# VectorE's and ScalarE's order in the last block of the first FFN

## The reference

```python
c  = cond(x)            # x @ W.T + 2 * (gated rank-16 LoRA, top 2 of 8 experts)
a  = sum_m term_m(c) @ fuse_m.T + approx_up(c) @ local.T
f  = (silu(c @ gate.T) * (c @ up.T)) @ down.T        # first FFN, 1248 hidden features
x1 = x + a + f
d  = x1 @ W2.T + b2 + 2 * (x1 @ A[slot]) @ B[slot]   # LoRA chosen per sequence
h1, h3 = lora_linear(d, w1), lora_linear(d, w3)      # second FFN, 1376 hidden features
out = x1 + lora_linear(silu(h1) * h3, w2)
```

## Time and profile before

| | |
|---|---|
| median of 3 runs | 448.58 us (448.51 to 448.97) |
| the profiled execution | 448.42 us |
| its span in the trace | 446.7 us |
| TensorE busy | 441.4 us, 99% |
| VectorE busy | 324.0 us, 73% |
| ScalarE busy | 212.2 us, 48% |
| TensorE's granted clock | 1.00 throughout |

### The profile page before, as it was taken

One profiled execution on the slowest core, in us unless ns is written; L12 is line 12 of the kernel. 1 busy time (PEld: TensorE's weight loads), 2 busy tenths in 40 slices (PEclk: granted clock), 3 DMA queues, 4 the chain that ended last, 5 costly groups with the idle time before them and its releaser, 6 DMA issues.

```text
span 446.7 us, 5568 instructions
## 1 busy us (share of the span) xinstructions
PE 441.4 (99%) x2009; PEld 363.5 (81%) x2009; DVE 324.0 (73%) x471; ACT 212.2 (48%) x324; POOL 29.3 (7%) x51
## 2 busy tenths in 40 slices
PE   8999999999999999999989999999999999999997
PEld 6788888888888888888778888888888888888886
DVE  5756699667989688896899248989853568887631
ACT  6364452345757447564565527365541124654300
POOL 1004100000001100005200000000000000000000
PEclk9999999999999999999999999999999999999999
DMA  8406800044574655657340010222201122121022
GB/s 301 132 0 195 201 0 1 12 119 117 117 190 118 147 133 121 145 138 198 109 150 6 18 48 18 70 66 61 74 2 41 57 91 66 48 66 53 1 102 87
DMA packets 20299, 40.44 MB, mean 91 GB/s; under 512 B 2672, under 2 KB 4736, under 8 KB 20272
## 3 DMA queue, kind: packets, MB, share of 16 engines
q1 hardware_dynamic: 16992, 32.51, 22.6%
q0 software_dynamic: 3280, 7.58, 9.7%
HBM read 37.98 MB, written 2.10 MB: 90 GB/s over the span
## 4 chain that ended last, share of the span: by engine, by line
PE 95%; DVE 3%; DMA 1%; ACT 0%; issue 0%; ACTq 0%
PE PS L1697 16%; PE PS L1698 16%; PE PS L1699 16%; PE PS L1562 15%; PE PS L1563 15%; PE PS L1564 15%; PE PS L1874 1%; DVE WU L938 1%; DMA X<-in_x 1%; DVE X L1180 1%; PE PS L1576 0%; PE PS L1922 0%; PE PS L1932 0%; PE PS L1933 0%; DVE S L1249 0%; DVE G L938 0%
## 5 line engine op out<-in xcount | busy, mean ns | idle before, releaser
L1697 PE MATMUL PS<-HT,WU 128*128 128x512 f32 x266 | 103.9, 391 | 1.3 <-DVE T L1123 1.0
L1698 PE MATMUL PS<-HT,WU 128*128 128x512 f32 x266 | 103.6, 389 | 0.0
L1699 PE MATMUL PS<-HT,WU 128*128 128x512 f32 x266 | 103.6, 389 | 0.0
L503 ACT ACTIVATE WU<-raw 128x256 fp32r<-128x256 f32 (+2 forms) x55 | 49.0, 897 | 31.0 <-PE PS L1699 15.1
L1697 PEld LDWEIGHTS PS<-HT,WU 128*128 128x128 f32 x266 | 50.0, 188 | 12.7 <-DVE T L1123 1.4
L938 DVE TENSOR_TENSOR WU<-raw,WU 128x256 fp32r<-128x256 f32 (+2 forms) x56 | 56.5, 1014 | 5.1 <-ACT WU L503 5.0
L1699 PEld LDWEIGHTS PS<-HT,WU 128*128 128x128 f32 x266 | 49.9, 188 | 10.5
L503 ACT ACTIVATE PS<-PS 128x512 f32<-128x512 f32 x46 | 26.8, 582 | 66.0 <-PE PS L1699 59.0
L1698 PEld LDWEIGHTS PS<-HT,WU 128*128 128x128 f32 x266 | 50.0, 188 | 10.0
L938 DVE TENSOR_TENSOR G<-T,G 128x1024 fp32r<-128x1024 f32 (+2 forms) x46 | 43.9, 967 | 12.2 <-ACT G L503 11.6
L503 ACT ACTIVATE G<-T 128x1024 fp32r<-128x1024 f32 (+2 forms) x47 | 39.8, 856 | 22.0 <-DVE T L1054 6.8
(11 more groups left out here) (170 smaller groups left out, 713.1 us busy)
## 6 DMA issues: line engine op xcount, KB each, us to landing
raw<-in_pieces SPq DMA_DIRECT2D x73, 256.0 KB, 3.0
raw<-in_parts SPq DMA_DIRECT2D x14, 512.0 KB, 3.6
raw<-in_parts POOLq DMA_DIRECT2D x14, 384.0 KB, 5.0
X<-in_x SPq DMA_DIRECT2D x8, 256.0 KB, 4.9
raw<-in_pieces SPq DMA_DIRECT2D x14, 128.0 KB, 2.8
out_x<-X SPq DMA_DIRECT2D x7, 256.0 KB, 2.0
su_raw<-in_stk_up POOLq DMA_DIRECT2D x6, 192.0 KB, 2.6
T<-in_lora_b POOLq DMA_DIRECT2D x16, 32.0 KB, 2.5
```

The source lines that it names most:

```text
L503: return nc.scalar.activation(o, i, ACT.Copy)
L1697: pe.matmul(bank, w[:, 1, cols], hi, start=start and kc == 0, stop=False, skip_group_check=not start)
L1698: pe.matmul(bank, w[:, 0, cols], low, start=False, stop=False, skip_group_check=not start)
L1699: mm = pe.matmul(bank, w[:, 0, cols], hi, start=False, stop=kc == 1, skip_group_check=not start)
```

## The change

It is an order of instructions alone; no instruction is added or taken away.

- On VectorE, `s13_lo` moves ahead of `x_out(12, "b")`, and `s2_lo(0)` moves behind `x_out(12, "c")`.
- On VectorE, `add_d1` moves ahead of `tail_lo(1)`, and `w_lo` of W2's third piece moves ahead of the two `tail_g_lo`.
- On ScalarE, `silu1(q, 0)` moves ahead of `tail_hi(1)`, and `w_hi` of W2's third and fourth pieces moves ahead of the two `tail_g_hi`.

```diff
@@ ScalarE, last(q)
                 s2_hi(3)
                 tail_hi(0)
+                silu1(q, 0)
                 tail_hi(1)
-                silu1(q, 0)
                 for k in range(2):
                     w_hi(P_W2 + k, W2[k])
                 silu1(q, 1)
+                for k in range(2, KC):
+                    w_hi(P_W2 + k, W2[k])
                 for h in range(HALVES):
                     tail_g_hi(C1 - 1, h)
-                for k in range(2, KC):
-                    w_hi(P_W2 + k, W2[k])
@@ VectorE, steady1(q) and last(q)
                     x_out(q, "a")
                     x_out(q, "d")
+                    if q == LAST - 1:
+                        s13_lo()
                     x_out(q, "b")
-                if q == LAST - 1:
-                    s13_lo()
-                    s2_lo(0)
 
             def last(q):
                 x_out(q - 1, "c")
-                s2_lo(1)
-                s2_lo(2)
+                for k in range(3):
+                    s2_lo(k)
                 add_b1(q)
                 s2_lo(3)
                 tail_lo(0)
+                add_d1(q)
                 tail_lo(1)
-                add_d1(q)
                 for k in range(2):
                     w_lo(P_W2 + k, W2[k])
                 mul1_1(C1 - 1)
                 mul0_1(C1 - 1)
+                w_lo(P_W2 + 2, W2[2])
                 for h in range(HALVES):
                     tail_g_lo(C1 - 1, h)
-                for k in range(2, KC):
-                    w_lo(P_W2 + k, W2[k])
+                w_lo(P_W2 + 3, W2[3])
```

## The result

The changed kernel takes 447.96 us in the median of 21 runs (447.60 to 448.52), the one before, run beside it, 448.89 us (448.44 to 449.34, 21 runs). The ratio is 0.9981, with a 95% interval of 0.9975 to 0.9987: about 0.85 us faster, 0.2%. The profiled execution took 447.73 us.

A forecast was written before the change was run, and what follows sets the result against it. TensorE, busy 99% of the span, bounds the kernel; only its stops in block 13 were in reach. 448.42 us minus 0.89 gives 447.53, plus 0.16 for the median 447.69, rounded 447.7; range 446.9 to 448.8.

The forecast's parts named there:

- Part 1: VectorE's queue from d to add_d in block 13: add_d starts 1.16 us earlier, 0.61 and 0.54 from two places.
- thin margin of 0.1 us: S2's third hi part on ScalarE is done at 221.58, VectorE wants it at 221.69.
- six long steps: VectorE's steps of 0.71 to 0.73 into or out of S rows: six in either order, against 0.61 otherwise.
- Part 2: TensorE in block 13: p7's stop goes, p3 loses 0.26 us instead of 0.60, p4 starts 1.16 us earlier.
- Part 3: From p4 to the tail: VectorE's queue sets mul0, new 0.17 us stop ahead of tail(0, 1), 0.89 us gained.
- W2's loads: Fourth piece issued at 223.84, landing after 2.9 us, copied near 227.40, before ScalarE is wanted at 228.18: free.
- the rival: ScalarE's tail_g_hi blocked behind a late W2 load: gain gone at 4.67 us landing, up to 450.71 us; chance 0.06.
- Part 4: Behind the tail: TensorE never stops and VectorE has room, so the 0.89 us lead is kept.
- the 2.06 us: Sum of TensorE's three stops in block 13, ahead of p7, p3 and p4: the most that can come back.

The follow-up runs named there:

- e1: Changed kernel with addition c and S2's first piece back where they stood before: median 448.88 us, 0.9997 of the kernel before.
- e2: Changed kernel with add_d behind both tail weights again: median 448.41 us, 0.9993 of the kernel before.
- e5: Changed kernel with S13 behind c, next to the three S2 rows: median 447.85 us, 0.9976 of the kernel before.
- e4: Changed kernel with W2's second lo part behind mul0 and the third behind tail_g_lo: median 447.75 us, 0.9970 of the kernel before.
- e6: Changed kernel with the load of W2's fourth piece issued about 1.9 us later: median 448.85 us, 1.0002 of the kernel before.
- e7: Changed kernel with W2's fourth load about 1.9 us later and its hi part behind tail_g_hi: median 448.26 us, 0.9986 of the kernel before.
- e8: Changed kernel with VectorE reordered (c behind b, W2's pieces after tail_g_lo) and ScalarE's fourth W2 hi part last: median 446.78 us, 0.9952 of the kernel before.
- e9: Changed kernel with S13 beside S2 rows, W2's second and third lo parts later, ScalarE's second silu earlier, fourth hi part behind tail_g_hi: median 447.38 us.
- e10: The kernel of e5 once more, against the changed kernel S13 behind c: 447.80 us in one run.

## Why the prediction was right

Forecast: 0.89 us less, 447.7 us. Measured: 0.85 by the ratio, 0.82 by the place, 447.96 us in a comparison in which the kernel before stood at 448.89 instead of 448.58. So the 0.26 us by which the time itself was missed come from the three runs that the forecast started from, and not from the mechanism. The prediction put the least difference that can be told from none at 0.2%; with 21 runs the interval is 0.06% wide to each side, so the gain is clear of none.

- *Part 1, VectorE's queue up to add_d.* 1.16 us forecast, 11.95 - 10.80 = 1.15 found. Both halves of it are there: the wait ahead of the third S2 row went, e1 brought it back and lost 0.53 of add_d; the tail weight behind add_d is e2, 0.60. The thin margin of 0.1 us of the S2 hi part held: it was over at 221.04 + 0.62 = 221.66, and VectorE, in steps of 0.61 from 220.54, wanted it at 221.76.
- *The six long steps.* They were six in both orders; e5 with four gained 0.23. The Trainium skill ("VectorE: DVE Perf Modes", section "Two Vector instructions with no wait between them") says that an instruction is held until all earlier ones have finished when its operands start in another group of 32 partitions. The trace agrees: 0.71 at a passage against 0.61 between rows that start alike, and in e5 S13 beside the S2 rows has the short step.
- *Part 2.* p7's stop gone; ahead of p3 0.28 lost, forecast 0.26; ahead of p4 0.67, forecast 0.65.
- *Part 3, the new stop.* It came where it was put, from the cause that was given (e4 removed it). Its size was a little off: 0.34 lost instead of 0.27. tail_g_lo's first half ended near 228.91 + 0.69 = 229.60 and the matmul started at 229.75, 0.15 later and not the 0.05 that add_d had shown. The restart cost 0.07 (229.75 to 230.05 is 0.30) and not 0.10. The 0.10 more and the 0.03 less are the difference between 0.89 and 0.82. Why this start took 0.10 us longer than the other no run shows.
- *W2's loads.* Landing after 2.8 us, copy over at 227.35, wanted at 228.24: hidden, as said. e6 and e7 confirm the condition and the price of the rival on both sides.
- *Part 4, the rest keeps it.* From block 12's add_d to the end of the span it is 446.7 - 213.65 = 233.05 before, 232.28 after (0.77 less, with spans given to 0.1) and 230.89 in e8 (2.16 less): nothing is given back behind the tail.

What I had not seen is how much stood ready beside this edit: I counted the 2.06 us as the ceiling, but did not ask for the order that reaches it.

## What to carry to other kernels

Where one engine works off a queue for another that must not stand, count the steps up to each instruction that is waited for: the gain of a move is the lead at the last of these waits, not at the nearest, and the same edit may have lengthened the queue ahead of a later one. Filler work that needs a load belongs behind what the critical engine waits for, on each engine it passes, since a queue worked off in order turns a late load into a stop. Compare small effects by a place in the trace behind the part that scatters, not by the total time alone.

## What the runs showed of the hardware that was not expected

- The scatter between the profiled executions comes from the first 100 us: block 0's add_d starts anywhere between 99.32 and 100.27 in thirteen traces of kernels that are alike up to there, while the next 114.24 us are the same in all of them.
- Loads of 256 KB that were issued 0.6 us apart, four in a row, landed after 2.6 to 2.8 us (first and second) and 3.8 to 4.5 us (third and fourth) in e5, e9 and e10; with 2 us between the first and the second they took 2.4 to 2.8 in the changed kernel, and the last of them up to 3.6 in others of the same spacing (e2, issued at 222.98). Whether the spacing is the cause stays open (see e9 and e10).
- A stop of TensorE costs more than its length: 0.33 us to the second matmul instead of 0.23 (0.30 ahead of tail(0, 1)), and then steps of 0.232 instead of 0.227, for the rest of the product behind p7, p3 and p4 and for some ten matmuls behind the stop of the tail.
